# Decoder on one core: in the attention rounds of four heads, the first products that run ahead move from in front of the value products to behind them

## What is computed

```
x = _layernorm(x + _L0_attn_ref(x, ...))      # 16 heads of 8, 512 keys
x = _layernorm(x + _L0_xattn_ref(x, ctx, ...)) # 16 heads of 8, 77 keys
...
a = softmax(einsum('bhsd,bhtd->bhst', q, k) * D ** (-0.5))
o = einsum('bhst,bhtd->bhsd', a, v)
```

## Time and profile before

| | |
|---|---|
| timed runs, median (lowest to highest) | 1805.57 us (1803.74 to 1805.57) |
| the profiled execution | 1804.04 us |
| its span, first to last instruction | 1802.1 us |
| mean granted TensorE clock | 0.898 of full |
| TensorE matmul (PE) busy | 1502.6 us, 83% |
| VectorE (DVE) busy | 1066.7 us, 59% |
| ScalarE (ACT) busy | 640.5 us, 36% |
| GpSimd (POOL) busy | 211.6 us, 12% |

### The profile page before, as it was taken

The page is one execution under the profiler, slowest core; times in us unless marked ns, Lnnn a source line. Parts: engine busy times, 40 slices in busy tenths (PEclk is TensorE's granted clock), DMA queues, the critical chain, the costliest instruction groups (busy, mean ns, idle before and its releaser), DMA issues. The chain is left out here.

```text
span 1802.1 us, 22144 instructions
## 1 busy us (share of the span) xinstructions
PE 1502.6 (83%) x8176; PEld 690.0 (38%) x8176; DVE 1066.7 (59%) x2630; ACT 640.5 (36%) x920; POOL 211.6 (12%) x227
## 2 busy tenths in 40 slices
PE   1699689994668889999988998998988679996885
PEld 0333244442223434446443233354436423334353
DVE  4696455456964667763544882555445556745354
ACT  1266252213325023332423663422212145552431
POOL 2000010001000534332000000000000103331000
PEclk9899689996978889998997998997987679998798
DMA  5000000003000010000002000000010000000000
GB/s 205 0 1 1 1 1 1 1 0 137 0 1 1 0 47 1 2 1 1 1 11 93 1 1 1 1 1 1 1 70 1 1 0 1 1 2 1 1 1 12
DMA packets 4074, 27.14 MB, mean 15 GB/s; under 512 B 384, under 2 KB 2432, under 8 KB 2944
## 3 DMA queue, kind: packets, MB, share of 16 engines
q1 hardware_dynamic: 2912, 25.22, 3.5%
q10 hardware_dynamic: 1056, 0.52, 0.1%
HBM read 25.21 MB, written 0.52 MB: 14 GB/s over the span
## 5 line engine op out<-in xcount | busy, mean ns | idle before, releaser
L833 DVE TENSOR_REDUCE maxima<-banks 128x1 f32<-128x512 f32 (+4 forms) x640 | 363.1, 604 | 107.7 <-PE banks L682 100.8
L977 ACT ACTIVATE big<-banks 128x1024 f32<-128x1024 f32 (+2 forms) x320 | 294.4, 960 | 264.8 <-PE banks L725 93.9
L710 PE MATMUL banks<-big 32*128 32x512 f32 (+6 forms) x1280 | 232.2, 612 | 17.2 <-DVE big L854 12.9
L682 PE MATMUL banks<-big 32*128 32x77 bf16 (+6 forms) x1024 | 157.9, 296 | 23.6 <-ACT big L238 6.1
L1444 DVE TENSOR_TENSOR big<-big,banks 128x512 f32<-128x512 f32 (+1 forms) x116 | 79.8, 688 | 151.8 <-PE banks L1357 146.4
L746 PE MATMUL banks<-big,v_heads 128*9 128x512 f32 (+7 forms) x1024 | 159.6, 569 | 6.3 <-ACT heads_out L893 3.2
L466 POOL TENSOR_TENSOR rstd<-mean_var,minus_half 128x4 f32<-128x4 f32 x34 | 34.9, 1025 | 1036.2 <-DVE mean_var L396 1036.2
L1419 ACT ACTIVATE big<-banks 128x512 f32<-128x512 f32 (+1 forms) x116 | 69.1, 596 | 178.6 <-PE banks L1356 178.4
L682 PEld LDWEIGHTS banks<-big 32*128 32x128 bf16 (+1 forms) x1024 | 57.1, 97 | 180.5 <-DVE maxima L833 92.8
L1387 PE MATMUL banks<-big,moe_weights 128*128 128x512 f32 (+1 forms) x232 | 118.9, 597 | 3.0 <-ACT big L1427 2.6
L710 PEld LDWEIGHTS banks<-big 32*128 32x128 f32 (+3 forms) x1280 | 72.8, 178 | 70.1 <-ACT big L977 23.7
(11 more groups left out here) (406 smaller groups left out, 2211.7 us busy)
## 6 DMA issues: line engine op xcount, KB each, us to landing
moe_weights<-in_moe SPq DMA_DIRECT2D x1, 4864.0 KB, 15.3
moe_weights<-in_moe SPq DMA_DIRECT2D x1, 4768.0 KB, 21.6
moe_weights<-in_moe SPq DMA_DIRECT2D x1, 3264.0 KB, 10.2
moe_weights<-in_l3x SPq DMA_DIRECT2D x1, 3072.0 KB, 9.9
late_weights<-in_l2x SPq DMA_DIRECT2D x1, 2048.0 KB, 7.9
moe_weights<-in_l SPq DMA_DIRECT2D x1, 1234.0 KB, 12.8
rows<-in_rows SPq DMA_DIRECT2D x1, 1152.0 KB, 8.1
late_weights<-in_turned SPq DMA_DIRECT2D x1, 1152.0 KB, 17.9
```

The costliest lines, as they stand in the source:

```text
L682: last = nc.tensor.matmul(RING[n % NR][:, x * klen:x * klen + last_key(t)], q[rows, t * P:(t + 1) * P], ks[rows, 0:last_key(t)], start=Tru ...
L710: last = nc.tensor.matmul(SC[pair % 2][0:size, j % 2, n0:S], ks[rows, i * P:i * P + size], q[rows, n0:S], start=True, stop=turned)
L833: nc.vector.tensor_reduce(dst, src, AX_X, ALU.max).then_inc(ring_free.up(), 1)
L977: nc.scalar.activation(E[pair % NEP][0:size, :, n0:S], SC[pair % 2][0:size, :, n0:S], ACT.Exp, scale=scale).then_inc(exp_ready.up(), 1)
```

## The change

In rounds of four heads (`halved` false) the two `soon` first products are issued after `values(pe, r - 1)` instead of before it. Where there is a turned maximum in the round, they still stand before it. Rounds of two heads keep their order, also the causal ones. No instruction is added or removed, the order of the ring's items is as it was, and so is the order on VectorE, ScalarE and GpSimd.

```diff
                 if r < R:
                     scores(pe, r)
                 turn_first = mask == "causal" and next_group(r) is not None
-                if not turn_first:
+                if halved and not turn_first:
                     for u in soon:
                         raw_scores(pe, u)
                 if 0 <= r - 1 < R:
                     values(pe, r - 1)
+                if not halved:
+                    for u in soon:
+                        raw_scores(pe, u)
                 if next_group(r) is not None:
                     turn_negmax(pe, next_group(r))
                 if turn_first:
```

## The result

| | before | after |
|---|---|---|
| median (lowest to highest) | 1804.91 us (1803.74 to 1805.57) | 1862.76 us (1861.61 to 1867.25) |
| profiled execution | 1804.04 us | 1867.25 us |
| its span | 1802.1 us | 1865.5 us |
| mean granted clock | 0.898 | 0.896 |
| PE busy | 1502.6 us, 83% | 1533.3 us, 82% |

Four runs each. The ratio is 1.0326, interval 1.0307 to 1.0345: slower by 57.9 us. The profiled execution of after is the longest of its four, which ran at clocks of 0.896 to 0.900, so its span is 63.4 us longer and not 57.9.

What follows compares the result with a forecast made beforehand. The prediction took TensorE's order of work to decide whether VectorE, with about 1 us slack per four rounds, is fed; 37.5 + 7.5 + 3.5 + 3.1 = 51.6 us on 1804.04 us gave 1856 us, range 1820 to 1875.

Steps and rivals of the forecast that it cites:

- the mechanism: Scores and values in one stretch feed VectorE nothing for longer than the ring's held maxima last, so it starves every round.
- Steady rounds of layers 0 and 2: Attentions of layers 0 and 2: four kinds of rounds lengthen by 1.03, 0.43, 0.91 and 0.53 us, 37.5 us in all.
- The gap: From the fourth first product to the next maximum: 2.46 us at least, against 1.7 us of work held for VectorE.
- the second rival: Scores start past the waiting fourth first product, so nothing is measured: 1804 us, up to 1812; chance 0.07.
- Rounds at half clock: First rounds of the stages, at the lower clock: taken at the same price as the others, with no row showing it.
- the third rival: Idle time drops the clock to 1.2 GHz, 52 rounds cost 90 us more, 1945 us; chance 0.05.
- Layer 3's first attention: Ring of two: values no longer cover holds; round kinds grow by 0, 0.56, 0.1 and 0.48 us, 7.5 us in all.
- Layer 3's second attention: Rounds 1 to 5: the turned maxima's wait for the ring, covered by values before, is uncovered; 5 x 0.7 = 3.5 us.
- Cross attentions: Layers 0 and 1: turned maxima brought in later, +0.39 us in rounds 1 and 2, 0.25 in rounds 3 to 5; 3.1 us.
- The first (faster): Values start earlier and VectorE never starves, so each group loses its 1.0 us idle time: 1791 us; chance 0.06.
- The fourth: Unseen slack in start-up rounds or stage ends gives back 15 to 30 us: 1826 us; chance 0.10.
- VectorE's idle time for first products: A sign to look for in the changed kernel: this idle time must grow by some 35 to 40 us.

Runs made afterwards that it cites:

- Experiment 6: Kernel 1 with rounds 0 to 7 of both stages kept in the order of the kernel before: 1828.67 us, 1.0131.
- kernel 1: The move made in the attentions of layers 0 and 2 alone, all other stages as in the kernel before: 1843.44 us, 1.0217.
- experiment 4: Ring of two banks instead of three in the attentions of layers 0 and 2: on kernel 1 1903.99 us, on the kernel before 1830.29 us.
- experiment 8: Kernel before, turned maxima ahead of values in layers 0 and 1's cross attentions: 1808.3 us; also moving masked values in layer 3's first attention, first rounds: 1809.26 us.

## Why the prediction was right, and where it was not

The forecast was 1856 us with 1844 to 1873 for the mechanism, the range 1820 to 1875; 1862.76 lies in both. The mechanism is the one foretold, and 51.6 us were expected for 57.9. That the total came so near is in part luck: in the profiled executions the steady rounds of layers 0 and 2 were priced 2.5 us too high, their early rounds 7.6 and the smaller stages 4.1 us too low, and the medians grew by 5.5 us less than those executions. A slip in the range: its terms, 42 us at the least, give 1846 and not 1844 us.

**Steady rounds of layers 0 and 2: right.** Predicted 3.29, 3.37, 3.98 and 4.61 us, measured 3.23, 3.34, 3.94 and 4.53, together 15.04 for 15.25. The gap was sized by its parts: 1.07, 0.98 and 0.43 us stand in the timeline of after, predicted 1.07 to 1.15, 0.97 and 0.42. VectorE's idle time is 0.86 us in plain rounds (about 0.8 predicted) and 1.34 after turned maxima (over 1). One part was misread. The 0.83 us from the start of a maximum to the first product that gets its bank is in the earlier trace rows the end of the values, and not the wait for the bank (in before):

```profile
111.00 0.19 PEld L710 LDWEIGHTS banks<-big 32*128 32x128 f32 x2 [0.60 <-ACT big L977]
...
112.06 1.05 PE L746 MATMUL banks<-big,v_heads 128*9 128x512 f32 x8
```

The first product of 113.03 follows them after 0.97 us, as the turned maxima do in the earlier trace rows after 0.98. Where it does wait for its bank, in after, the time is 0.74 us (118.86 to 119.60). The 0.86 us at 122.45, held against the second rival, is such an end of values too. And the exponentials "don't set the pace" after the change only: in before, a weight load of the scores waits 0.60 us for one at 111.00, and the values of that round start 1.96 us after its scores at 110.10. By the measured kinds, 6 x 0.97 + 7 x 0.40 + 7 x 0.87 + 6 x 0.46 = 17.5 us per stage, against 18.7 predicted.

**Rounds at half clock: the step that failed.** They were taken at the same price, with no row behind it. The stages grew by 21.8 and 20.8 us, 4.3 and 3.3 more than steady rounds make. In layer 0 it is all in rounds 1 to 3: 6.08, 5.45 and 6.44 us, before 4.69, 2.78 and 4.37, so 6.1 us where steady rounds would make 1.7. Round 1 is at the lower clock in both kernels and alone costs 1.39 us instead of 0.40, since scores and values in the gap are nearly twice as long. The timeline of after:

```profile
91.68 1.90 PE L746 MATMUL banks<-big,v_heads 128*9 128x512 f32 x8
...
94.14 2.48 DVE L833 TENSOR_REDUCE maxima<-banks 128x1 f32<-128x512 f32 x4 [2.97 <-PE banks L682]
```

Values take 1.90 us as in the earlier trace rows, and VectorE stands 2.97 us for its next first product. Before, these values, of round 2, took 1.05 us, since the upper clock had come by then. So in rounds 2 and 3 the new order pays for the gap at half clock and for having kept the clock low. Experiment 6 shows this with the early rounds put back: the clock rises as before and 8.8 us of layer 0's 21.8 are gone, of which steady prices explain 1 x 0.97 + 2 x 0.40 + 2 x 0.87 + 2 x 0.46 = 4.4. In layer 2 the excess is in rounds 0 to 2: 3.26, 6.07 and 5.25 us, before 2.64, 4.72 and 2.51. Round 0 holds no move, so part of it is only that the lower clock lay elsewhere, and kernel 1 with the same order took 2.64, 5.93 and 3.34 us: there the steady prices nearly hold (+18.1 for 17.5). So layer 0's excess is shown to come with the order, layer 2's not. Of the third rival the changed kernel has this late rise, in a few rounds instead of 52; in the steady rounds the clock didn't fall.

The Trainium skill, "TensorE: Matmul & The Clock Gate", section "A second HAM failure mode: psum-queue depth-cycling", says that short idle times of TensorE between its groups of matmuls, in a kernel that cycles through PSUM banks, can make the clock go back and forth. The trace of after does not show this in the steady state (83% busy, 12.50 of 15.05 us, at 1.00); the late order with a ring of two in experiment 4 does (0.95, then 0.61).

**Layer 3's first attention: the mechanism right, 10.3 us for 7.5.** The four kinds were predicted at 0, +0.56, +0.1 and +0.48; measured 0 (4.33 in both), +0.71 (3.82 to 4.53), +0.25 (4.62 to 4.87) and +0.48 (4.43 to 4.91). Second and third are both 0.15 too low. In the timeline of after:

```profile
1589.95 0.40 PE L682 MATMUL banks<-big 32*128 32x512 bf16 x2
...
1591.21 0.38 PE L695 MATMUL banks<-ident_bf,negmax 128*128 128x128 bf16 x4 [0.87 <-DVE maxima L833]
...
1598.82 0.85 PE L748 MATMUL banks<-big,v_heads 128*32 128x384 f32 x8
1599.61 0.40 PE L682 MATMUL banks<-big 32*128 32x512 bf16 x2
...
1600.93 0.84 PE L682 MATMUL banks<-big 32*128 32x512 bf16 x2
```

First products follow 0.79 us after the start of the 384-column values. I had put these values at 0.65 us, from what they added between two pairs of first products; in before, sums follow them after 0.67 us. The 0.12 us between the two is most of the 0.15. What makes it is open: behind values of 512 columns in layer 0 first products and turned sums both follow after 0.98 us. The turned maxima now wait 0.87 us for the ring instead of 0.51, 0.36 more for 0.37 predicted. The later pair starts 1600.93 - 1599.61 = 1.32 us after the earlier, spread over 0.84 us, so the held pair that the prediction took from a round without values is there.

**Layer 3's second attention, 4.3 us for 3.5.** Its rounds 1 to 5 grew by 0.96, 0.80, 0.82, 0.85 and 0.82 us, taken as 0.7 each: 0.1 of it may be the same change from values to first products, which I did not measure here.

**Cross attentions, 3.7 us for 3.1.** Layer 0's rounds grew by 0.43, 0.29, 0.28, 0.42 and 0.42, predicted 0.39, 0.39 and three times 0.25. VectorE's wait in after:

```profile
254.90 0.86 DVE L833 TENSOR_REDUCE maxima<-banks 128x4 f32<-128x308 f32 x2 [1.43 <-PE banks L682]
255.68 0.68 DVE L854 TENSOR_TENSOR big<-big,banks 128x512 f32<-128x512 f32 x1
```

It now stands for the first products, 1.43 us against 0.33, and brings in the turned maxima the moment its own are done: the releaser changed as foretold.

**The rivals.** The first (faster) needed VectorE not to starve; it does. The second (scores past the waiting first product) is refuted by 119.60 and 119.61: both the load of the first product and the scores start once VectorE has freed a bank, in the steady rounds shown. The third is above. The fourth, a slack that gives back half, wasn't there: the start-up rounds took as much or more, not less.

**A sign that was sized wrong.** VectorE's idle time for first products was to grow by 35 to 40 us; by the page it grew by 78.3. That is more than the kernel's own 57.9 us, so part of it is only a change of releaser, as in the cross attentions: 1.43 us for 0.33 in a round that grew by some 0.4. The page's idle time by releaser is no price.

## What to carry to other kernels

Where a ring of PSUM banks couples TensorE to a reader, compare two numbers for each stretch in which the in-order engine feeds the ring nothing: what the reader holds when it begins (banks less what has passed, times its time for one) and how long it lasts until the next item lands. Here 1.7 against 2.46 us foretold 15.25 us per group for 15.04 measured; and one item left inside the stretch took away four fifths of the loss (8.2 for 39.5 us). Price the rounds that run at the lower clock by themselves, and ask whether the change still lets the engine work there without a break: in layer 0 of the changed kernel starved rounds went with a rise of the clock some ten microseconds later, in layer 2 of kernel 1 they did not.

## What was not expected of the hardware

TensorE's busy share alone does not tell its clock. It had 1.00 at 67% busy and at 83% in after, fell from 0.95 at 78% (23.31 of 30 us) in the late order with two banks, and was still at 0.54 when 91% busy in the late order with short values:

```profile
105.00:110.00 5.00, 4.55 (x20) 0.97 (x20) 2.15 (x5) 1.94 (x2) 0.00 (x0) 0.54 0.00 0
```

At the lower clock the same matmuls also fill more time, so a high share there is partly an effect of the clock. And in experiment 8 a stage made shorter by 0.7 us was followed by a stretch with a lower clock that cost six times as much, in both kernels that have it; a gain of this size can't be read from one stage alone.
